# Attention softmax with split float32: joined TensorE passes, a VectorE share, and probabilities normalised on GpSimd

## What is computed

```python
x = rmsnorm(hidden_states, ln1_w)
q = einsum('bsh,dh->bsd', x, q_w).reshape(b, s, NH, QHD)[..., :NOPE]
k, v = ...                                  # (b, s, 16, 128) each
scores = einsum('bqnd,bknd->bnqk', q, k) * scale
scores = where(causal, scores, -1e9)
p = softmax(scores, axis=-1)
attn = einsum('bnqk,bknd->bqnd', p, v).reshape(b, s, NH * VD)
hid = hidden_states + einsum('bsd,hd->bsh', attn, o_w)
```

## Time and profile before

| | |
|---|---|
| median of 3 runs | 785.31 us (783.17 to 785.88) |
| profiled execution | 785.51 us, its span 783.6 us |
| busy, share of the span | PE 95%, PEld 74%, DVE 73%, ACT 59%, POOL 37% |
| granted TensorE clock, mean | 0.992 |

### The profile page before, as it was taken

One profiled execution on the slowest core, in us unless ns is written; L12 is line 12 of the kernel. 1 busy time (PEld: TensorE's weight loads), 2 busy tenths in 40 slices (PEclk: granted clock), 3 DMA queues, 4 the chain that ended last, 5 costly groups with the idle time before them and its releaser, 6 DMA issues.

```text
span 783.6 us, 12388 instructions
## 1 busy us (share of the span) xinstructions
PE 741.8 (95%) x4153; PEld 583.5 (74%) x4164; DVE 574.4 (73%) x1222; ACT 462.5 (59%) x1018; POOL 292.2 (37%) x182
## 2 busy tenths in 40 slices
PE   6996989999989999999999999999998999999996
PEld 2443544445546899999999999998877888888985
DVE  1689999998899678748775776687665555647476
ACT  3599888878765467727673675476662433425251
POOL 5004999999779711201210211001432222313130
PEclk9997999999999999999999999999999999999999
DMA  7121343443232200000010110001229251515101
GB/s 291 46 74 54 111 123 102 118 93 115 70 90 60 76 28 28 28 28 28 30 54 1 39 42 28 21 21 61 82 72 241 75 161 48 171 48 156 47 0 54
DMA packets 24876, 59.03 MB, mean 75 GB/s; under 512 B 3536, under 2 KB 5072, under 8 KB 24704
## 3 DMA queue, kind: packets, MB, share of 16 engines
q1 hardware_dynamic: 24832, 58.47, 25.0%
HBM read 57.21 MB, written 1.25 MB: 75 GB/s over the span
## 4 chain that ended last, share of the span: by engine, by line
PE 70%; DVE 12%; ACT 5%; issue 5%; POOL 5%; DMA 1%; DVEq 0%; SPq 0%; POOLq 0%; ACTq 0%
PE ps L1024 17%; PE ps L1026 17%; PE ps L1025 17%; PE ps L540 6%; POOL m_ring L400 4%; DVE m_ring L899 4%; PE ps L1181 3%; PE ps L446 2%; PE ps L489 2%; PE ps L498 2%; PE ps L544 2%; DVE e_aw L1971 2%; DVE e_sg L1965 1%; POOL m_ring L392 1%; DVE m_ring L904 1%
## 5 line engine op out<-in xcount | busy, mean ns | idle before, releaser
L540 PE MATMUL ps<-m_ring,ident 128*128 128x512 f32 x256 | 121.5, 602 | 5.2 <-POOL m_ring L400 4.5
L1135 POOL TENSOR_TENSOR a_wl<-raw,a_wh 128x1024 fp32r<-128x1024 f32 (+1 forms) x16 | 32.0, 2001 | 239.6 <-ACT a_wh L1321 239.6
L1645 POOL TENSOR_TENSOR e_wl<-raw,e_wh 128x512 fp32r<-128x512 f32 (+1 forms) x55 | 57.8, 1060 | 155.1 <-ACT e_wh L1775 84.7
L400 POOL TENSOR_TENSOR m_ring<-m_ring,m_c_sb 128x1024 f32<-128x1024 f32 x40 | 94.4, 2367 | 14.0 <-DVE m_ring L899 12.5
L392 POOL TENSOR_TENSOR m_ring<-m_du,m_b_sb 128x1024 f32<-128x1024 f32 x31 | 73.5, 2370 | 57.2 <-DVE m_ring L886 57.2
L540 PEld LDWEIGHTS ps<-m_ring,ident 128*128 128x128 f32 x256 | 47.1, 192 | 50.3 <-issue 38.2
L1024 PE MATMUL ps<-a_rowsh,e_wh 128*128 128x512 f32 x200 | 78.3, 392 | 0.4 <-DVE e_sg L1965 0.2
L1025 PE MATMUL ps<-a_rowsl,e_wh 128*128 128x512 f32 x200 | 77.9, 389 | 0.0
L1026 PE MATMUL ps<-a_rowsh,e_wl 128*128 128x512 f32 x200 | 77.9, 389 | 0.0
L899 DVE TENSOR_TENSOR_SCAN m_ring<-m_first,ps 128x1024 f32<-128x1024 f32 x32 | 72.8, 2276 | 5.3 <-ACT ps L748 2.5
L1333 ACT ACTIVATE a_p<-a_p,a_nmax 128x128 f32<-128x128 f32 (+1 forms) x128 | 57.1, 447 | 29.3 <-DVE a_nmax L1426 28.0
(11 more groups left out here) (220 smaller groups left out, 2136.3 us busy)
## 6 DMA issues: line engine op xcount, KB each, us to landing
raw<-in_expert_w SPq DMA_DIRECT2D x30, 384.0 KB, 3.5
raw<-in_attn_w SPq DMA_DIRECT2D x20, 512.0 KB, 3.3
m_c_sb<-bc SPq DMA_DIRECT2D x40, 256.0 KB, 3.5
m_b_sb<-bc SPq DMA_DIRECT2D x32, 256.0 KB, 4.1
e_wb<-wt SPq DMA_DIRECT2D x20, 256.0 KB, 4.5
e_wb<-wt SPq DMA_DIRECT2D x4, 448.0 KB, 5.3
e_wb<-wt SPq DMA_DIRECT2D x4, 384.0 KB, 4.6
e_wb<-wt SPq DMA_DIRECT2D x4, 320.0 KB, 4.5
```

The source lines that it names most:

```text
L400: nc.gpsimd.tensor_tensor(split(slot(n)), split(slot(n)), c_sb[:, k % C_BUFS:k % C_BUFS + 1, :].to_broadcast([P, 2, HALF]), ALU.mult).then ...
L540: nc.tensor.matmul(ps[:, Y_BANK + c, :], ident[:, :], slot(n)[:, c * HALF:(c + 1) * HALF], start=False, stop=False, skip_group_check=True) ...
L1135: nc.gpsimd.tensor_tensor(w[1][:, j, cols], raw[:, j, cols], w[0][:, j, cols].bitcast(F32), ALU.subtract).then_inc(w_done, 1)
L1645: nc.gpsimd.tensor_tensor(w[1][:, k, cols], raw[:, k, cols], w[0][:, k, cols].bitcast(F32), ALU.subtract).then_inc(low, 1)
```

## The change

In scores() the first query half takes two passes in place of three: low by high as before, and one of 256 columns that moves the high and the low part of k through with the same weights (qh), into blocks 0 and 3. In weigh() the same is done for the last keys: pTh and pTl move together, into blocks 1 and 2 of the bank. For this k and pT are kept as one tensor with both parts. The share that now stands in another block is added by VectorE: in maxes() block 3 and the mask are first added into p, then the 256-column half is reduced, then the 128-column half; in low_o() a second, 128-column add follows the subtraction. The two multiplications of normalize() move to GpSimd (`normalize` in its program), with rs broadcast along the columns; the reciprocal stays on VectorE (`one_over`, in place of every call of normalize in its program). In GpSimd's order, unit n + 1, n + 2, n + 3 are normalised, then the weights' split is done, then unit n + 4.

```diff
@@ -95,10 +95,12 @@
             ol = ctx.enter_context(nc.sbuf_tensor("a_ol", [P, GH, T], F32R))
             sb("gap0", [P, EC * BATCH * (NTAP - 1)])
             self.o = ctx.enter_context(nc.sbuf_tensor("a_oh", [P, GH, T], F32R)), ol
-            self.k, self.q, self.rows = (parts(name, [P, 2, T]) for name in ("k", "q", "rows"))
+
+            self.k = ctx.enter_context(nc.sbuf_tensor("a_k", [P, 2, 2, T], F32R))
+            self.q, self.rows = (parts(name, [P, 2, T]) for name in ("q", "rows"))
             self.p = sb("p", [P, BATCH, 3 * P])
             sb("gap1", [P, HALF])
-            self.pT = parts("pT", [P, 2, 3 * P])
+            self.pT = ctx.enter_context(nc.sbuf_tensor("a_pT", [P, 2, 2, 3 * P], F32R))
             sb("gap2", [P, HALF])
             self.v = parts("v", [P, 2, TT, 2 * HD])
 
@@ -1026,6 +1028,14 @@
     return nc.tensor.matmul(out, ll, rh, start=False, stop=stop, skip_group_check=True)
 
 
+def joined_passes(nc, out, lhs, both, start, stop):
+
+
+    lh, ll = lhs
+    nc.tensor.matmul(out[:, 0, :], ll, both[:, 0, :], start=start, stop=False, skip_group_check=True)
+    return nc.tensor.matmul(out, lh, both, start=False, stop=stop, skip_group_check=True)
+
+
 def attention_block(nc, ctx, d, keep, ps, space, rows):
 
     def sb(name, shape, dt=F32):
@@ -1036,7 +1046,8 @@
 
     hid, ident, identb, mask = (keep[k] for k in ("hid", "ident", "identb", "mask"))
     raw = keep["raw"]
-    w, q, k_, v, p, pT, o = space.w, space.q, space.k, space.v, space.p, space.pT, space.o
+    w, q, v, p, o = space.w, space.q, space.v, space.p, space.o
+    k_, pT = ([x[:, part] for part in range(2)] for x in (space.k, space.pT))
     nmax, sums, rs = (sb(f"a_{n}", [P, 4, 2]) for n in ("nmax", "sums", "rs"))
 
     ld_w = keep["ld_attn"]
@@ -1044,6 +1055,7 @@
     r_ready, rh_done, r_free = sem("r_ready"), sem("rh_done"), sem("r_free")
     s_ready, max_done, exp_done = sem("s_ready"), sem("max_done"), sem("exp_done")
     rs_done, norm_done = sem("rs_done"), sem("norm_done")
+    masked, o_joined = sem("masked"), sem("o_joined")
     pT_ready, ph_done, pl_done = sem("pT_ready"), sem("ph_done"), sem("pl_done")
     o_ready, oh_done, ol_done = sem("o_ready"), sem("oh_done"), sem("ol_done")
 
@@ -1135,11 +1147,28 @@
             nc.gpsimd.tensor_tensor(w[1][:, j, cols], raw[:, j, cols], w[0][:, j, cols].bitcast(F32),
                                     ALU.subtract).then_inc(w_done, 1)
 
-        with pool.Fori(1, NG) as g:
+        def normalize(n, b):
+            pool.wait_ge(rs_done, n + 1)
+            for t, cols, count in ((0, slice(0, P), P), (1, slice(P, 3 * P), 2 * P)):
+                nc.gpsimd.tensor_tensor(p[:, b, cols], p[:, b, cols], rs[:, b, t:t + 1].to_broadcast([P, count]),
+                                        ALU.mult).then_inc(norm_done, 1)
+
+        def step(g, j, cols):
+            n = g * (GH * BATCH) + j * BATCH
+            for b in range(1, BATCH):
+                normalize(n + b, b)
+            pack(g * GH + (GH + j), j, cols)
+            if not (isinstance(g, int) and g == LAST and j == GH - 1):
+                normalize(n + BATCH, 0)
+
+        normalize(0, 0)
+        for j in range(GH):
+            step(0, j, slice(0, PACK))
+        with pool.Fori(1, LAST) as g:
             for j in range(GH):
-                pack(g * GH + j, j, slice(0, PACK))
+                step(g, j, slice(0, PACK))
         for j in range(GH):
-            pack(NG * GH + j, j, OUT_COLS)
+            step(LAST, j, OUT_COLS)
 
     def tensor(pe):
         def project(n, u, j_next, pair_next, tile0):
@@ -1168,13 +1197,15 @@
                 pe.wait_ge(max_done, n - 1)
             bank, t0 = ps[:, 2 + b % 2, :], b * SEQ
 
-            for first, keys, cols in ((t0, P, slice(0, P)), (t0 + P, SEQ, slice(P, 3 * P))):
-                mm = three_passes(nc, bank[:, cols], [x[:, j % 2, first:first + P] for x in q],
-                                  [x[:, j % 2, t0:t0 + keys] for x in k_], first == t0, True)
+            blocks = bank.rearrange("p (a c) -> p a c", c=P)
+            joined_passes(nc, blocks[:, 0:4:3, :], [x[:, j % 2, t0:t0 + P] for x in q],
+                          space.k[:, :, j % 2, t0:t0 + P], True, True)
+            mm = three_passes(nc, bank[:, P:3 * P], [x[:, j % 2, t0 + P:t0 + SEQ] for x in q],
+                              [x[:, j % 2, t0:t0 + SEQ] for x in k_], False, True)
             mm.then_inc(s_ready, 1)
 
         def turn(n, b):
-            pe.wait_ge(norm_done, n + 1)
+            pe.wait_ge(norm_done, 2 * n + 2)
             if not (isinstance(n, int) and n < 2):
                 pe.wait_ge(pl_done, n - 1)
             for blk in range(3):
@@ -1190,8 +1221,9 @@
             bank, cols = ps[:, 6 + b % 2, :], slice((j % 2) * HD, (j % 2 + 1) * HD)
             vs = [[x[:, j // 2, 2 * b + kt, cols] for x in v] for kt in range(2)]
             three_passes(nc, bank[:, 0:SEQ], vs[0], [x[:, b % 2, 0:2 * P] for x in pT], True, False)
-            three_passes(nc, bank[:, P:SEQ], vs[1], [x[:, b % 2, 2 * P:3 * P] for x in pT], False,
-                         True).then_inc(o_ready, 1)
+            blocks = bank.rearrange("p (a c) -> p a c", c=P)
+            joined_passes(nc, blocks[:, 1:3, :], vs[1], space.pT[:, :, b % 2, 2 * P:3 * P], False,
+                          True).then_inc(o_ready, 1)
 
         def outputs(g):
 
@@ -1421,20 +1453,21 @@
             if not (isinstance(n, int) and n < BATCH):
                 dve.wait_ge(pT_ready, n + (1 - BATCH))
 
-            nc.vector.memset(rs[:, b, :], 0.0)
-            for t, cols in ((0, slice(0, P)), (1, slice(P, 3 * P))):
-                m = nc.vector.tensor_tensor_reduce(out=p[:, b, cols], in0=ps[:, 2 + b % 2, cols], in1=mask[:, cols],
+            nc.vector.tensor_tensor(p[:, b, 0:P], ps[:, 2 + b % 2, 3 * P:4 * P], mask[:, 0:P], ALU.add
+                                    ).then_inc(masked, 1)
+            for t, cols, more in ((1, slice(P, 3 * P), mask[:, P:3 * P]), (0, slice(0, P), p[:, b, 0:P])):
+                if t == 0:
+
+                    dve.wait_ge(masked, n + 1)
+                    nc.vector.memset(rs[:, b, :], 0.0)
+                m = nc.vector.tensor_tensor_reduce(out=p[:, b, cols], in0=ps[:, 2 + b % 2, cols], in1=more,
                                                    op0=ALU.add, op1=ALU.min, scale=-1.0, scalar=-MASKED,
                                                    accum_out=nmax[:, b, t:t + 1])
             m.then_inc(max_done, 1)
 
-        def normalize(n, b):
+        def one_over(n, b):
             dve.wait_ge(exp_done, n + 1)
             nc.vector.reciprocal(rs[:, b, :], sums[:, b, :]).then_inc(rs_done, 1)
-            dve.wait_ge(rs_done, n + 1)
-            for t, cols in ((0, slice(0, P)), (1, slice(P, 3 * P))):
-                m = nc.vector.tensor_scalar(p[:, b, cols], p[:, b, cols], rs[:, b, t:t + 1], None, ALU.mult)
-            m.then_inc(norm_done, 1)
 
         def low_p(n, b):
             dve.wait_ge(ph_done, n + 1)
@@ -1445,7 +1478,10 @@
             toks = slice(b * SEQ, (b + 1) * SEQ)
             dve.wait_ge(oh_done, n + 1)
             nc.vector.tensor_tensor(o[1][:, j, toks], ps[:, 6 + b % 2, 0:SEQ], o[0][:, j, toks].bitcast(F32),
-                                    ALU.subtract).then_inc(ol_done, 1)
+                                    ALU.subtract).then_inc(o_joined, 1)
+            dve.wait_ge(o_joined, n + 1)
+            late = o[1][:, j, b * SEQ + P:(b + 1) * SEQ]
+            nc.vector.tensor_tensor(late, late.bitcast(F32), ps[:, 6 + b % 2, SEQ:SEQ + P], ALU.add).then_inc(ol_done, 1)
 
         def add_output(g):
             if isinstance(g, int) and g == 0:
@@ -1469,7 +1505,7 @@
-        normalize(0, 0)
+        one_over(0, 0)
...
```

More of the change, by code:

```diff
@@ L1483, in step @@
             if not units:
-                normalize(n + 1, 1)
+                one_over(n + 1, 1)
                 maxes(n + 2, 2)
@@ L1488, in step @@
                 low_p(n + 1, 1)
-                normalize(n + 2, 2)
-                normalize(n + 3, 3)
+                one_over(n + 2, 2)
+                one_over(n + 3, 3)
                 low_o(n, j, 0)
@@ L1521, in step @@
             low_o(n + 3, j, 3)
-            normalize(n + BATCH, 0)
+            one_over(n + BATCH, 0)
             fill(5)
```

## The result

The changed kernel took 791.39 us (median of 4 runs, 790.4 to 791.97) beside 784.90 us of the kernel before on the same chip, a ratio of 1.0072 (95% interval 1.0042 to 1.0102): 6.5 us slower. The profiled executions took 791.69 and 785.51 us, spans 789.8 and 783.6.

What follows compares the result with a forecast made beforehand. TensorE's own queue was taken to bound attention (274 of 784 us). Waits of 11.5 + 7.9 + 2.6 + 1.3 + 1.7 = 25.0 against 14.1 gained made it 10.9 slower: 796.2 us, range for 8 in 10 784 to 805, own range 790 to 804.

Steps and rivals of the forecast that it cites:

- The joining: Scores and weighted sums on TensorE: five weight loads for six, 0.11 us each, 64 + 64 times, 14.1 us gained.
- The rival that it saves nothing: TensorE: 128-column passes cost half a 256-column pass, so no time is taken out; 798 us, chance 0.05.
- GpSimd's pair: Normalisation on GpSimd: two multiplies of 128 and 256 columns take 0.46 + 0.74 = 1.20 us; probabilities come 0.70 later.
- turn(n + 2)'s wait of 0.72: TensorE's transposes of unit n + 2 wait 0.72 us for late probabilities in all 16 steps, 11.5 us.
- turn(n)'s of 0.61: TensorE's transposes of unit n wait 0.61 us for late probabilities, 13 times, 7.9 us.
- VectorE's sums: VectorE's added work: 0.20 us for the mask add in maxes(), 0.32 for the second add in low_o().
- outputs(): TensorE's output passes wait for low_o(n + 3) 0.85 us more, 3 times, 2.6 us.
- Starting again: TensorE after waits at transposes: next work starts 0.31 us after them instead of 0.25; 0.06 x 29 = 1.7 us.
- The last step: Attention's end: less work beside it, so transposes and the first output sum wait longer, an estimated 1.3 us.
- The weights' split: GpSimd's queue: the 2.41 us split between normalising n + 3 and n + 4 ends early enough to delay nothing.
- The cheap broadcast: GpSimd multiplies near 0.55 us a pair; weigh(n + 2) waits 0.64 instead; 786.3 us, up to 790 at 0.9; chance 0.15.
- The expensive multiply: GpSimd's two multiplies cost as its TENSOR_SCALAR row, 0.65 us more at 29 places, 19 us, 815; chance 0.06.

Runs made afterwards that it cites:

- the version without sums: The changed kernel with VectorE's and ScalarE's calls reordered and a finer wait in outputs(), but VectorE's two added sums left out: 770.83 us, 0.9821 of the kernel before.
- the reciprocals earlier: The changed kernel with two reciprocals moved up in VectorE's order, ahead of fill(1)'s low part and of low_o(n + 3): 790.03 us, 1.0066 of the kernel before.
- the joined passes alone: The changed kernel without VectorE's two added sums and with normalisation back on VectorE: 781.99 us, 0.9952 of the kernel before.

## Why the prediction was right, and which terms were off

The direction and the cause held: TensorE gains from 128 loads, and waits at the transposes give more back. The size was 10.9 us where 6.2 was measured between the profiled executions.

- **The joining** (14.1): confirmed, at 0.10 a load for 0.11. There are 4036 loads for 4164, and the version without sums gained 13.8, some 13 of it by the loads. The load behind a joined pass's own still comes 0.11 later, as between two short passes:

```profile
369.19 0.19 PEld L1036 LDWEIGHTS ps<-a_k,a_qh 128*128 128x128 f32 x1
369.30 0.19 PEld L1026 LDWEIGHTS ps<-a_k,a_qh 128*128 128x128 f32 x1
```

  The rival that it saves nothing is refuted: a pass of 128 or of 256 columns costs its weight load here. The isolated times of the Trainium skill ("TensorE: Matmul & The Clock Gate", Back-to-back issue gap), by which the gain would be nil, do not fit this kernel. The same section says itself that they count too little at few columns in a stream of weight loads and matmuls, and gives some 81 ns for 128 columns there. The traces here have 110 ns.
- **GpSimd's pair** (1.20) is the term that was mis-sized most: it measured 0.97, 400 ns and 613 ns for 460 and 740. The hand-over was 0.07 to 0.08, as taken. I priced the multiply by the subtraction that writes fp32r, as the nearest row; no row told me that the form with a broadcast column is shorter. It lay in the gap between my cheap case (0.55, or up to 0.9) and my own range (1.05 to 1.40). By the same working it turns turn(n + 2)'s wait of 0.72 into 0.49 (measured 0.43) and turn(n)'s of 0.61 into 0.38 (measured 0.36). At 29 places 0.23 us is 6.7.
- **weigh(n + 2)** I let wait only in the cheap rival. It waits 0.17 beside the other two, 2.6 us that my sum left out. The prediction has both chains, 0.72 at turn(n + 2) in the forecast and 0.64 at weigh(n + 2) in the rival ("no slack"; its terms as written add up to 0.62), but never sets them side by side. While turn(n + 2) is 0.72 late it covers the other. With the real pair it is 0.49 late, and the 0.64 counts, however much of it falls to the transposes. Measured are 0.43 + 0.17 = 0.60 in the change, and 0.65 at weigh(n + 2) alone with the reciprocals earlier. Corrected for both, the sum is 16 x 0.64 + 13 x 0.38 + 2.6 + 1.3 + 1.7 = 20.8 given back for 14.1, 6.7 slower; measured 6.2. That it comes so near is in part luck, since terms are off in both directions: the loads are worth 1 us less, and the waits are 28.
- **VectorE's sums** (0.20 and 0.32): right. The mask add's successor starts 0.20 later (370.63 to 370.83). low_o() takes 0.66 (372.80 to 373.46) where it took 0.33.
- **outputs()** (0.85 more each): 338.39 shows 1.06 of idle time for 0.24 before, 0.82 more. **Waits**: 28 on GpSimd for the 29 forecast; turn(n) of the last step doesn't wait. **The step** was to be 0.5 longer and is 0.28 longer. **Starting again** (1.7): the next work comes 0.30 after late transposes, where it came after 0.24 (turn(n)) and 0.27 (turn(n + 2)) before, some 1.1 in all. **The last step** (1.3) can't be set beside one measured number: the 1.1 from the first transposes of the last step but one to the end holds its waits and its saved loads together.
- **The weights' split** in GpSimd's queue delays nothing, as said: 375.22 to 377.64, and the next pair starts at 381.93 when its reciprocal comes.
- **The cheap broadcast** came half true: cheaper than thought, and with weigh(n + 2) in front of TensorE as the rival had it, but not in place of the waits on GpSimd. By the time alone the two can't be told apart: 791.4 lies at the low end of my own range (790) and just over the rival's upper end (790). The 28 waits on a_p decide. The reciprocals earlier show that rival in pure form: with turn's waits removed, weigh(n + 2) takes them over, and 5 us of loss remain where the rival had 1. The rest is fill(1)'s 0.31 in 11 steps, 3.4 us, for which it had no term. The expensive multiply (1.85) is refuted by the 0.97, and VectorE's sums were not cheaper than taken.

What I did not ask was whether the loss belonged to the change or to the order left around it. The runs say the order: with three moved calls on VectorE, one on ScalarE and a finer wait the same arithmetic is 10 us faster than the kernel before. That needs GpSimd's part: without it the same orders end at 793.26.

## What to carry to other kernels

When work is taken from the engine that bounds, list the slack of every operand that it asks for in a step: the saving is worth little more than the smallest slack allows (here 0.11 us a step of 0.88, with the joined passes alone), unless the order on the feeding engines moves with it. Price all chains together, since one that is second by 0.1 us (0.64 beside 0.72 here) takes over when the first is shortened, and try such edits in pairs: here 1.4 and 2.6 us alone were 10.8 together. Read such small gains from distances inside the trace; two medians of executions that differ by 1 to 3 us don't show them. An engine may place next what TensorE needs next (a reciprocal, the low part of transposed data) ahead of what is only stored.

## What was not expected of the hardware

GpSimd's float32 multiply by one column broadcast over the row takes 400 ns for 128 and 613 ns for 256 columns, 1.66 ns a column and some 190 ns besides. Its subtraction that writes fp32r takes 742 ns for 256 and 2418 for 1024, 2.18 a column. The output type doesn't make the difference: in the same trace an addition of two full operands with a float32 output takes 791 ns for 256 columns, and the scan's float32 multiply takes 2366 for 1024, as long as the subtraction.

```profile
L1689 POOL TENSOR_TENSOR hid<-hid,x 128x256 f32<-128x256 f32 x8 | 6.0, 791 | 0.0
...
L402 POOL TENSOR_TENSOR m_ring<-m_ring,m_c_sb 128x1024 f32<-128x1024 f32 x40 | 94.4, 2366 | 13.9 <-DVE m_ring L901 12.4 <-PE ps L542 1.3
```

That leaves the operand that doesn't advance along the row as the likely reason. No run has the same multiply with a full second operand, so it isn't shown.
